# Two exchanges in a hand-written attention schedule, and a reciprocal placed ahead of a maximum

## What is computed

```
h = _rms(x, ln_w)
q = (h @ wq).reshape(B, S, 32, 64);  k, v = (h @ wk), (h @ wv) as (B, S, 8, 64)
q, k = _rope(q, k)                       # 4 query heads share one key head
scores = causal(einsum('bqhd,bkhd->bhqk', q, k) / 8)
attn = softmax(scores, -1)
o = einsum('bhqk,bkhd->bqhd', attn, v)
x = x + o @ wo                           # then 4 of 16 experts per token
```

## Time and profile before

| | us |
|---|---|
| time, median of 3 runs | 2113.06 (2111.1 to 2116.01) |
| the profiled execution | 2112.84 |
| its span | 2111.0 |
| 64-wide attention, prologue to drain | about 803 to 1733 |
| one steady round | 28.45 |

### The profile page before, as it was taken

One profiled execution on the slowest core, in us unless ns is written; L12 is line 12 of the kernel. 1 busy time (PEld: TensorE's weight loads), 2 busy tenths in 40 slices (PEclk: granted clock), 3 DMA queues, 4 the chain that ended last, 5 costly groups with the idle time before them and its releaser, 6 DMA issues.

```text
span 2111.0 us, 32365 instructions
## 1 busy us (share of the span) xinstructions
PE 1810.6 (86%) x10666; PEld 1224.6 (58%) x10666; DVE 1320.8 (63%) x3898; ACT 1097.9 (52%) x2886; POOL 917.8 (43%) x1013
## 2 busy tenths in 40 slices
PE   4989899867888845999999999999999994799994
PEld 2656678733434323666666666666667664555552
DVE  5675545446686855777877777787777766522222
ACT  3323244226565533767666676666667661344441
POOL 3991000002221001555555555555555551588884
PEclk9999899958999986999999999999999995899997
DMA  5000020000001010000000000000000007255556
GB/s 152 1 1 2 1 60 1 1 0 1 1 1 41 1 43 1 1 1 1 1 1 1 1 1 1 1 1 1 1 1 1 1 1 276 73 82 84 82 84 163
DMA packets 61426, 61.71 MB, mean 29 GB/s; under 512 B 13136, under 2 KB 58320, under 8 KB 61264
## 3 DMA queue, kind: packets, MB, share of 16 engines
q0 software_dynamic: 15360, 20.98, 6.3%
q1 hardware_dynamic: 45904, 38.65, 5.7%
HBM read 40.48 MB, written 19.14 MB: 28 GB/s over the span
## 4 chain that ended last, share of the span: by engine, by line
PE 62%; DVE 21%; issue 8%; ACT 4%; POOL 3%; DMA 2%; SPq 0%; ACTq 0%; POOLq 0%; DVEq 0%
PE banks L1799 7%; PE banks L1818 6%; PE banks L1787 5%; PE banks L1777 5%; PE banks L1808 5%; DVE wide_x L1052 4%; PE banks L1995 3%; PE banks L1830 3%; PE banks L1621 3%; PE banks L1872 3%; PE banks L1847 2%; DVE con L1063 2%; POOL wdT L725 2%; PE banks L1683 2%; PE banks L1892 2%
## 5 line engine op out<-in xcount | busy, mean ns | idle before, releaser
L1777 PE MATMUL banks<-wide_k,wide_q 128*128 128x512 f32 (+3 forms) x1024 | 316.3, 391 | 7.2 <-DVE con L1033 3.9
L657 POOL TENSOR_TENSOR wugT<-wugT,con 128x512 f32<-128x512 f32 (+1 forms) x256 | 246.4, 984 | 5.1 <-DVE con L1016 2.1
L1406 ACT ACTIVATE wugT<-wugT,con 128x512 f32<-128x512 f32 (+1 forms) x256 | 169.9, 665 | 134.5 <-DVE con L1033 134.5
L1777 PEld LDWEIGHTS banks<-wide_k,wide_q 128*128 128x128 f32 x1024 | 167.1, 191 | 90.5 <-issue 35.8
L668 POOL TENSOR_TENSOR attn<-attn 128x320 f32<-128x320 f32 x128 | 111.4, 871 | 238.4 <-DVE attn L1004 238.4
L1033 DVE CUSTOM_DVE_ANT_0 wugT<-banks,wide_mask 128x512 f32<-128x512 f32 (+1 forms) x256 | 158.2, 618 | 86.1 <-PE banks L1777 82.7
L1063 DVE TENSOR_REDUCE con<-banks 128x1 f32<-128x512 f32 x256 | 163.6, 680 | 52.6 <-PE banks L1860 52.2
L1818 PE MATMUL banks<-late,xnT 128*128 128x384 f32 x512 | 192.1, 499 | 3.2 <-ACT xnT L1436 2.0
L1052 DVE TENSOR_TENSOR wide_x<-attn,wide_x 128x256 fp32r<-128x256 f32 (+1 forms) x256 | 174.1, 720 | 31.0 <-ACT wide_x L1440 31.0
L1799 PE MATMUL banks<-attn 128*64 128x256 f32 x1280 | 166.5, 389 | 0.0
L1995 PE MATMUL banks<-w,late 128*128 x320 | 156.5, 612 | 2.4 <-ACT late L1533 1.7
(11 more groups left out here) (311 smaller groups left out, 4191.0 us busy)
## 6 DMA issues: line engine op xcount, KB each, us to landing
w<-in_L_ffn_w_dram SPq DMA_DIRECT2D x32, 256.0 KB, 6.1
late<-in_L_ffn_w_dram SPq DMA_DIRECT2D x16, 256.0 KB, 6.2
y_rows<-wqkv1T SPq DMA_DIRECT2D x1, 2176.0 KB, 7.9
x<-in_L_attn_x_dram SPq DMA_DIRECT2D x4, 512.0 KB, 8.9
late<-in_L_ffn_wq_dram SPq DMA_DIRECT2D x2, 1024.0 KB, 7.3
late<-in_L_ffn_wo_dram SPq DMA_DIRECT2D x1, 2048.0 KB, 8.4
h_rows<-wugT SPq DMA_DIRECT2D x1, 2048.0 KB, 7.0
y_rows<-x SPq DMA_DIRECT2D x1, 2048.0 KB, 13.1
```

The costliest lines, as they stand in the source:

```text
L657: nc.gpsimd.tensor_tensor(p, p, rinv[:, m:m + 1].to_broadcast([P, n]), ALU.mult).then_inc(at.sem["norm"], 1)
L1406: nc.scalar.activation(at.prob(m)[:, 0:n], at.prob(m)[:, 0:n], ACT.Exp, bias=negmax[:, m:m + 1], scale=-1.0, accum_out=rowsum[:, m:m + 1]) ...
L1777: ins = nc.tensor.matmul(sbank[:, 0:keys], wide_q[:, side, i, qcols], wide_k[:, side, w, 0:keys], start=(w == 0), stop=(w == 1))
```

## The change

Three exchanges of places. In slots 1 and 4 the `qkv` entry stands ahead of the `project` entry. In slot 12 `turn_qk` 4 stands behind turn 5 and values 0 to 3 instead of ahead of them. In `dve_work`, the reciprocal for the unit two slots back stands ahead of the wait for the scores and their maximum instead of behind the maximum. Nothing is added or removed. With the new order in the list, the two banks that `qkv` and `project` share are also assigned differently.

```
-                1: [("project", -1, 1), ("qkv", 1, 0)],
+                1: [("qkv", 1, 0), ("project", -1, 1)],
...
-                4: [("low", 1, 0), ("project", -1, 2), ("qkv", 1, 1)],
+                4: [("low", 1, 0), ("qkv", 1, 1), ("project", -1, 2)],
...
-                12: [("low", 1, 3), ("turn_qk", 1, 4), ("turn", 0, 5), ("values", 0, 0), ("values", 0, 1), ("values", 0, 2),
-                     ("values", 0, 3)],
+                12: [("low", 1, 3), ("turn", 0, 5), ("values", 0, 0), ("values", 0, 1), ("values", 0, 2), ("values", 0, 3),
+                     ("turn_qk", 1, 4)],
...
                     if kind == "scores":
+                        if a >= at.behind:
+                            invert(n, a - at.behind)
+                        elif reached(n):
+                            invert(n - 1, at.units + a - at.behind)
                         v.wait_ge(at.sem["s_ps"], n * at.units + a + 1)
...
                         nc.vector.tensor_tensor_reduce(at.prob(a)[:, 0:kk], sc, wide_mask[:, S - kk:S], -1.0, 3.0e38, ALU.add, ALU.min,
                                                        negmax[:, a:a + 1]).then_inc(at.sem["max"], 1)
-                        if a >= at.behind:
-                            invert(n, a - at.behind)
-                        elif reached(n):
-                            invert(n - 1, at.units + a - at.behind)
```

## The result

The changed kernel takes 2101.8 us (median of 14 runs, 2098.91 to 2108.39), the kernel before beside it 2113.17 us (14 runs, 2104.38 to 2120.91). The ratio is 0.9954, with a 95% interval of 0.9939 to 0.9969: faster by 0.46%, 11.4 us. The forecast was 2115 us. The profiled execution of the changed kernel took 2098.91 us, its span is 2097.1 us.

The account below looks back on a forecast made before the run. TensorE was taken as busiest, with a DVE, POOL and ACT chain setting project 3 in 30 equal rounds of 28.45 us. Terms of -0.05, +0.05 and +0.07 made +0.07 us a round, +2 us: 2115 us, range 2097 to 2131.

Parts of the forecast that it names:

- rival B: Front stretch gains more, with PE running freely to project 3: 6 to 16 us faster, around 2101; chance 22%.
- The sum: Adds the terms of the steady rounds: +0.07 us a round, 30 rounds, +2 us; bounds -6 and +13 us.
- Part 1: Slot 1, qkv 0 ahead of project 1: PE stands 0.66 us for the staging copy, yet qkv 0 loads earlier.
- Part 2: Slot 4 and first reciprocals: normalisations and low part 0 end sooner; with Part 1, -0.05 us a round (-0.25 to +0.15).
- rival E: Reciprocals gain through POOL; PE waits for none of its normalisations, so this meant no change; not counted apart.
- Part 3: Slot 12, turn_qk 4 behind the values: its 1.08 us gap moves whole to turn_qk 5; +0.05 us a round.
- Part 4: Reciprocals ahead of the maxima: the two around low part 2 delay exponential 11; +0.07 us a round (0 to +0.24).
- A: Both big stalls, slots 7 and 12, go and nothing replaces them: 1.32 us a round, 40 us, 2073; chance 6%.
- C: Front stretch: low part 0 stays caught between two normalisations, 1.88 us; 21 us slower, 2134; chance 13%.
- D: Reciprocals cost their full 157 ns ahead of the maxima of three chains: 10 us slower, 2123; chance 15%.

Follow-up runs that it names:

- d1: The changed kernel with two unused 128x512 copies added on VectorE between the attention and the norm behind it; 2109.75 us, ratio 0.9978.
- d2: The kernel before with three unused 128x512 copies and one of 128x128 added on VectorE ahead of the norm behind the attention; 2113.12 us, ratio 0.9998.
- e5: Kernel before with qkv ahead of project in slots 1 and 4, and reciprocals ahead of the maximum only in slots 2, 3 and 4; 2104.38 us.
- e6: Kernel before with qkv ahead of project in slots 1 and 4, and reciprocals ahead of the maximum except in slots 2, 3 and 4; 2132.51 us.
- e1: Kernel before with only the exchanges in slots 1 and 4 (qkv ahead of project); 2124.15 us, ratio 1.0052.
- e2: Kernel before with only the exchange in slot 12 (turn_qk 4 behind values 0 to 3); 2112.52 us, ratio 0.9990.
- e4: Kernel before with the exchanges in slots 1 and 4 and all reciprocals early, slot 12 as before; 2097.11 us, ratio 0.9918.
- e3: Kernel before with only the reciprocals moved ahead of the maxima; 2109.00 us, ratio 0.9975.

## Why the prediction was right or wrong

It was wrong: next to no change was forecast (+2 us, too little to be measured), and the kernel is faster by 11.4 us. The measured time is in the range, where rival B had it (around 2101), but that is luck: B's mechanism gave only 4.5 us, less than its 6 to 16, and the rest came from a stretch of which no rival spoke.

**The step that failed is "The sum".** It says that the steady rounds are all that the edits change, 30 times, and so it has no term for anything behind the attention. The router stretch got 6.3 us shorter there, by the clock, and that is more than half of the 11.4. No edit causes it: d1 takes it away and d2 brings half of it with a few copies. From the trace of before it could have been seen that this stretch runs at a granted clock of 0.50 for 17 us while PE is busy without a break. A stretch that runs wholly at the lower of the clock's two levels can only get shorter by it. Whether it would, and by how much, could not have been read from that trace; the runs show up to 6.3 us, against a sum of 2, and a term on that side should have moved the chances towards faster.

**The steps inside the round**, by the runs:

- Part 1. Wait for the staging copy, taken as 0.66: 0.69 us. From the load of scores 0, qkv 0 was to load 1.91 us later, rope 0 to start at 3.55, the first normalisation at 5.41. Measured 1.90, 3.50 and 5.35 (1226.34, 1227.94 and 1229.79 less 1224.44). Right.
- Part 2, the mis-sized term. Taken at -0.05 us a round, with -0.25 as the favourable end. The normalisations take 3.04 us, not 3.2, since low part 0 is now asked for while the third runs, and no normalisation stands behind it that it could hold up; rope 1 starts at 8.79, not 9.0; maximum 5 at 10.19, not 10.4; project 3 at 11.79 (a load at 1236.23), where 12.06 was before. That is 0.27 a round in the changed kernel. In e5, without the other edits' costs, it is 0.31 (28.453 - 28.141), a little past the favourable end. The chain through DVE, POOL and ACT set project 3 as argued: PE still waits for the output copy there, 0.51 instead of 0.71 us. One reading of the kernel before was inexact: its low part 0 is asked for (1236.62) while the second normalisation runs, the third begins at 1237.1, so there a normalisation did stand behind it.
- That unit 2's reciprocal must come ahead of maximum 4 for low part 0 to be free was said in part 2, and no run tests it alone. What e5 and e6 show is how much hangs on the three together: 0.85 us a round between the reciprocals of units 0 to 2 early and late, with those of the other slots alike (29.05 - 28.20, 28.98 - 28.14). In e1 and e6 POOL waits 0.29 us for unit 0's and 0.63 for unit 1's, the one behind maximum 3. For unit 2's it does not wait there: its second and third normalisation follow each other without a gap. The prediction priced the reciprocals' own cost in the streams and wrote under rival E that their earlier arrival at POOL is worth nothing, while its own part 2 used it. It is the heart of the change: without it the exchanges cost 0.53 us a round.
- Part 3. "The gap moves whole to turn_qk 5, +0.05": 1.14 us for ACT L1398 instead of 1.08 for DVE L1052, and e2 costs 0.05. Together with the other edits it costs 0.10 (e4 to the changed kernel). ACT's queue has the order that was counted out; from exponential 11 to the load of turn_qk 5 it took 2.78 us (1245.47 to 1248.25), 2.77 was worked out.
- Part 4. Reciprocals elsewhere +0.07: 0.06 by e4 against e5. That they gain 0.08 when they are the only edit (e3) was not in its bounds, which went from nothing upwards; the gain sits in the shorter normalisations and low part 0.

So the steps from the kernel before to e5 (-0.31), on to e4 (+0.06) and to the changed kernel (+0.10) make the -0.15 us a round. They add up because they are steps between the same four kernels, so this is no second check of the account.

**The rivals.** A's two stalls stayed (0.51 and 1.14 us). C's mechanism is real: it is what the exchanges in slots 1 and 4 do alone (e1). In the changed kernel the third normalisation has begun when low part 0 is asked for. D falls: a reciprocal in a chain costs 0.07 to 0.08 us between starts also after the change (maximum 5 starts at 1234.63, the reciprocal ahead of it at 1234.55), though its record says 0.15. The Trainium skill (VectorE: DVE Perf Modes, The TRN2 errata) measures a fixed term of about 150 cycles in the duration of a single instruction. The length of the record here agrees with that; what the stream pays is half of it. On the sharing between POOL and DVE (the Trainium skill, GPSIMD Engine Reference, 1. Specifications) the trace agrees with it: the same pair of low-part instructions takes 1.88, 1.10 and 0.63 us beside two normalisations, the end of one, and none.

## What to carry to other kernels

Where two engines take turns at a shared resource, price an edit by the order in which their instructions meet, not by each one's own duration: an exchange that costs 0.53 us a round alone and a reciprocal that gains 0.08 gave a gain of 0.25 together, because one closed the gap that the other opened. In a queue with a single buffer behind it, a stall in front of an instruction is worth little until the consumer's own queue is counted: moving turn_qk 4 behind all the values moved 1.08 us and gained nothing, while placing it in the middle and taking one item out of ACT's queue ahead of its copy gained 0.40 us a round (28.20 to 27.80). Before a gain of a few microseconds is put down to an edit, compare the stretches that the edit doesn't touch, with their granted clock.

## What the runs showed of the hardware

The same 96 small matmuls and transposes, behind an idle time of 12.03 or 12.04 us in all kernels but d1 and d2, took 14.1, 17.2 or 20.3 us, the same for one kernel in both of its traces (20.35 and 20.34; 14.08 and 14.07). In the kernel before the clock stayed at 0.50 (1.2 GHz) for the 20.35 us, with PE busy without a break, and so it did in d1. In the changed kernel and in d2 it rose to 1.00 (2.4 GHz) and fell back to 0.50 before the stretch was over, also while PE was busy without a break. A lengthening of the idle time by 0.43 us turned the shortest into the longest, one of 1.23 us the longest into the middle one.

The two DVE instructions of a low part, each with two SBUF inputs, took 0.63 us with POOL idle, 1.10 in the changed kernel, where they met only the end of one normalisation, and 1.88 in the kernel before and in e1, where a further one stood behind it. The three normalisations took 3.04 us in the changed kernel and 3.36 in the kernel before. A reciprocal of one column has a record of 0.15 us, and the next instruction on DVE starts 0.07 to 0.08 us after it.
